# GpSimd's early work given to ScalarE and VectorE, with the maxima of the next head in three attention groups

## The reference, cut to what matters

```
x = x + gnn(layernorm(x))            # (x - mean) / sqrt(var + 1e-5)
x = x + ffn(layernorm(x))
def gat(x, W, a_src, a_dst, bias):   # per head
    h    = x @ W
    al_s = sum(h * a_src);  al_d = sum(h * a_dst)
    e    = leaky_relu(al_s[src] + al_d[dst], 0.2)
    ex   = exp(e - segment_max(e, dst)[dst])
    out  = segment_sum(h[src] * ex / segment_sum(ex, dst)[dst], dst)
# gnn: layer 1 has 4 heads of 512 and an elu, layer 2 one head of 768
# ffn: router, top 2 of 8 experts of capacity, experts and a shared expert
```

## Time and profile before

| what | value |
|---|---|
| median of 3 executions | 1455.62 us (1454.12 to 1456.59) |
| profiled execution | 1458.8 us, its span 1457.0 us |
| granted TensorE clock, mean | 0.932 |
| busy: PE, PEld | 1255.7 us (86%), 817.3 us (56%) |
| busy: DVE, ACT, POOL | 919.4 us (63%), 583.2 us (40%), 293.8 us (20%) |
| chain that ended last | PE 54%, DVE 23%, DMA 7%, ACT 6%, POOL 5%, issue 5% |

### The profile page before, as it was taken

The page is one execution under the profiler, slowest core; times in us unless marked ns, Lnnn a source line. Parts: engine busy times, 40 slices in busy tenths (PEclk is TensorE's granted clock), DMA queues, the critical chain, the costliest instruction groups (busy, mean ns, idle before and its releaser), DMA issues.

```text
span 1457.0 us, 18197 instructions
## 1 busy us (share of the span) xinstructions
PE 1255.7 (86%) x7084; PEld 817.3 (56%) x7084; DVE 919.4 (63%) x1694; ACT 583.2 (40%) x1015; POOL 293.8 (20%) x198
## 2 busy tenths in 40 slices
...
GB/s 168 53 171 167 16 56 138 112 18 102 133 109 29 110 151 96 35 64 90 41 124 188 160 86 58 42 172 43 97 66 1 63 204 183 174 193 189 174 59 29
DMA packets 71009, 151.55 MB, mean 104 GB/s; under 512 B 10789, under 2 KB 34853, under 8 KB 70298
## 3 DMA queue, kind: packets, MB, share of 16 engines
...
...
HBM read 117.78 MB, written 34.59 MB: 105 GB/s over the span
## 4 chain that ended last, share of the span: by engine, by line
PE 54%; DVE 23%; DMA 7%; ACT 6%; POOL 5%; issue 5%; SPq 1%; POOLq 0%; DVEq 0%; ACTq 0%
PE PS L1684 41%; PE PS L1812 7%; DVE sb L1327 3%; DVE sb L1254 3%; POOL sb L780 3%; DVE sb L1348 2%; DMA sb<-in_L_gnn_W_dram 2%; DVE sb L1363 2%; DVE sb L1356 2%; DMA sb<-aa_d 2%; DVE sb L1210 2%; PE PS L1714 1%; PE PS L1807 1%; DVE sb L1399 1%; DVE sb L1388 1%
## 5 line engine op out<-in xcount | busy, mean ns | idle before, releaser
L1684 PE MATMUL PS<-sb,sb 128*125 128x384 f16 (+8 forms) x4404 | 789.2, 340 | 55.9 <-DVE sb L1231 24.5
L1684 PEld LDWEIGHTS PS<-sb,sb 128*125 128x125 f16 (+3 forms) x4404 | 545.2, 129 | 286.8 <-issue 70.6
L1812 PE MATMUL PS<-sb,sb 125*128 125x375 f16 (+1 forms) x1440 | 261.0, 342 | 0.0
L1812 PEld LDWEIGHTS PS<-sb,sb 125*128 125x128 f16 x1440 | 140.0, 98 | 118.9 <-issue 8.2
L797 POOL TENSOR_TENSOR sb<-sb,sb 125x768 f32<-125x768 f32 x10 | 18.0, 1841 | 672.2 <-DMA sb<-in_x_dram 672.2
L949 ACT ACTIVATE sb<-sb 125x375 f32<-125x375 f32 (+1 forms) x150 | 81.6, 544 | 116.4 <-DVE sb L1348 116.1
L1528 DVE SCALAR_TENSOR_TENSOR sb<-sb,sb 128x2304 f16<-128x2304 f32 x27 | 68.8, 2557 | 84.3 <-ACT sb L1085 84.3
L1348 DVE SCALAR_TENSOR_TENSOR sb<-sb,sb,sb 125x375 f32<-125x375 f32 (+1 forms) x150 | 95.7, 639 | 30.6 <-ACT sb L943 30.5
L1714 PE MATMUL PS<-sb,sb 125*125 125x500 f16 x286 | 75.0, 422 | 36.1 <-ACT sb L928 23.4
L780 POOL TENSOR_TENSOR sb<-sb,sb 128x768 f32<-128x768 f32 x32 | 79.1, 2494 | 122.0 <-ACT sb L903 75.2
L943 ACT ACTIVATE sb<-sb,sb 125x375 f32<-125x375 f32 (+1 forms) x150 | 93.7, 628 | 24.2 <-DMA sb<-aa_d 24.2
...
## 6 DMA issues: line engine op xcount, KB each, us to landing
...
```

The lines of the kernel that those rows point to most:

```text
L1684: ins = M(out_, lhs(a), rhs(b), start=first and a + b == 0, stop=last and a == 1)
L1812: ins = M(PS[:, t, 0:n], hb[:, i, pa, 128 * c:128 * c + 128], P[:, i, pb, lo:lo + n], start=i == 0 and pa + pb == 0, stop=i == NT - 1 and ...
```

## The change

- GpSimd does no early work but constants: the source differences go to ScalarE, one ACTIVATE of 125x125 for each of the 171 edge columns (`differences`), the sums of W2 rows to VectorE as one multiply-and-sum of 128x768 each (`v2_sums`, 32), the lo weights of head 1 to VectorE (6).
- ScalarE normalises x, with scale and bias from VectorE (MS1 is minus mean times scale).
- Six slots for rows of W2 instead of three; the loads of head 1's weights stand ahead of `chain_row(0)` in SP's order.
- In the heads: maxima in g2, g3 and g4 (3, 3, 4) instead of two in each of g2 to g6; the shift at group 7 instead of 10; the next head's P from g9 instead of g11; W1_AT from g5 on; other counts of P calls. Masks are loaded one after the other, and the last two weight rows after the shifts.

```diff
@@ tables
-        CUR_STEPS = [[3, 3, 2, 2, 2, 2, 2, 2, 2, 0, 0, 0, 0, 0, 0],
-                     [2, 2, 2, 2, 2, 2, 2, 0, 0, 0, 0, 0, 0, 0, 0],
...
+        CUR_STEPS = [[2, 2, 2, 2, 2, 2, 2, 2, 2, 2, 0, 0, 0, 0, 0],
+                     [1, 1, 0, 0, 0, 2, 2, 2, 2, 1, 0, 0, 0, 0, 0],
+                     [1, 1, 0, 0, 0, 2, 2, 2, 2, 1, 0, 0, 0, 0, 0],
+                     [1, 1, 1, 1, 1, 2, 2, 2, 2, 0, 0, 0, 0, 0, 0]]
-        MAX_STEPS = [0, 0, 2, 2, 2, 2, 2, 0, 0, 0, 0, 0, 0, 0, 0]
+        MAX_STEPS = [0, 0, 3, 3, 4, 0, 0, 0, 0, 0, 0, 0, 0, 0, 0]
-        NEXT_STEPS = [[0, 0, 0, 0, 0, 0, 0, 0, 0, 0, 0, 2, 2, 2, 2],
...
+        NEXT_STEPS = [[0, 0, 0, 0, 0, 0, 0, 0, 0, 1, 2, 2, 2, 2, 2],
+                      [0, 0, 0, 0, 0, 0, 0, 0, 0, 1, 2, 2, 2, 2, 2],
+                      [0, 0, 0, 0, 0, 0, 0, 0, 0, 2, 3, 3, 3, 3, 3]]
+        V2_H = [0, 1, 1, 2, 1, 2, 1, 2, 2, 2]
+        V2_H1 = [0, 0, 0, 3, 1, 1, 1, 1, 1, 1]
-        W1_AT = {3: 0, 4: 1, 5: 2, 6: 3, 7: 4, 8: 5}
-        ROW_AT, SHIFT_AT = 1, 10
+        W1_AT = {5: 0, 6: 1, 7: 2, 8: 3, 9: 4, 10: 5}
+        ROW_AT, SHIFT_AT = 1, 7
@@ gpsimd: differences, products and lo weights of head 1 taken out
-            pool.wait_ge(s_slo, 1)
-            for i in range(NT):
-                a, b = OLP * i, min(OLP * (i + 1), KA)
-                nc.gpsimd.tensor_tensor(OL[:, a:b, :], iot[:, :].unsqueeze(1).to_broadcast([T, b - a, T]),
...
@@ scalar
+            def differences(q):
+                if q == 0:
+                    act.wait_ge(s_keys, 2)
+                a, b = OLP * q, min(OLP * (q + 1), KA)
+                for t in range(a, b):
+                    ins = A(OL[:, t, :], iot[:, :], ACT.Identity, bias=SLO[:, t:t + 1], scale=-1.0)
+                ins.then_inc(s_od, 1)
+
+            def normalise(n):
+                act.wait_ge(s_ms1, n + 1)
+                for i in range(*PIECES[n]):
+                    A(XA[:, i, :], XA[:, i, :], ACT.Identity, bias=MS1[:, i:i + 1], scale=SD[:, i:i + 1]
+                      ).then_inc(s_xn, 1)
+
             deviation(0)
+            normalise(0)
             deviation(1)
+            normalise(1)
+            differences(0)
...
             for i in range(NT):
+                if i == 2:
+                    differences(1)
                 if i == XF:
                     deviation(2)
+                    normalise(2)
...
             for i in range(NT):
                 h_hi(0, i)
-                if i >= 4:
-                    v2_sum(summed)
-                    summed += 1
+                if 1 <= i <= 5:
+                    differences(i + 1)
             w1_hi(1, range(KD))
 
+            for q in range(7, 9):
+                differences(q)
             for c in range(NC):
+                if c == 3:
+                    differences(9)
@@ vector
-                for i in range(a, b):
-                    V.tensor_scalar(XA[:, i, :], XA[:, i, :], MV1[:, i, 0:1], SD[:, i:i + 1], ALU.subtract,
-                                    ALU.mult).then_inc(s_xn, 1)
+                V.scalar_tensor_tensor(MS1[:, a:b], MV1[:, a:b, 0], -1.0, SD[:, a:b], ALU.mult, ALU.mult
+                                       ).then_inc(s_ms1, 1)
...
+            def v2_sums(n):
+                for k in range(summed[0], min(summed[0] + n, 2 * NCH)):
...
+                    V.tensor_tensor_reduce(VJ[:, :], WV[ch % 6][:, :], A2R[:, a, :], SW, 0.0, ALU.mult, ALU.add,
+                                           V2F[:, ch, a:a + 1]).then_inc(s_va, 1)
...
             for q in range(NT):
                 h_lo(0, q)
-                if q >= 2:
+                if 2 <= q <= 6:
                     source_onehots(q)
+                v2_sums(V2_H[q])
+            w1_lo(1, range(KD))
...
             chain_row(0)
-            pair_onehots(range(T0, ET))
+            for a in range(T0, ET, OLP):
+                for q in range(7, NT):
+                    if a <= OLP * q < a + OLP:
+                        source_onehots(q)
+                pair_onehots(range(a, min(a + OLP, ET)))
+                v2_sums(1 if a + OLP < ET else 0)
...
@@ sync
-                    load_masks(h + 1, 2)
+                    for t in range(2, 5):
+                        load_masks(h + 1, t)
                     if h + 2 < H:
                         load_al(h + 2)
                         load_w1_rows(h + 2, range(2))
-                    load_masks(h + 1, 3)
-                    load_masks(h + 1, 4)
+                    store_h1(NB * h)
                     if h + 2 < H:
-                        load_w1_rows(h + 2, range(2, KD))
-                    store_h1(NB * h)
+                        load_w1_rows(h + 2, range(2, 4))
                     chain_shift(h + 1)
+                    if h + 2 < H:
+                        load_w1_rows(h + 2, range(4, KD))
```

More of the change, by code:

```diff
@@ L133, in build @@
     MV1 = at(o_ct + 12800, [T, NT, 2], F32)
-    WV = [at(o_y + 3072 * b, [128, D], F32) for b in range(3)]
-    A2R = at(o_y + 9216, [128, 2, D], F32)
-    VP = [at(o_y + 15360 + 3072 * b, [128, D], F32) for b in range(4)]
-    assert o_y + 15360 + 4 * 3072 <= o
+    MS1 = at(o_ct + 12928, [T, NT], F32)
+    WV = [at(o_y + 3072 * b, [128, D], F32) for b in range(6)]
+    A2R = at(o_y + 18432, [128, 2, D], F32)
+    VJ = at(o_y + 24576, [128, D], F32)
+    assert o_y + 27648 <= o
     W2S = [at(o_w2s + 3072 * i, [128, 2, D], F16) for i in range(9)]
@@ L317, in build @@
         s_ml = [sem(f"masks_loaded{b}") for b in range(2)]
-        s_vp = sem("v2_product_made")
+        s_wv = [sem(f"w2_rows_in_slot{b}") for b in range(3, 6)]
         s_va = sem("v2_sum_made")
@@ L531, in _ @@
                 load_v2(ch)
-            for q in range(3, NT):
+            for q in range(3, 6):
+                load_xt(0, q)
+                load_v2(q)
+            for q in range(6, NT):
                 load_xt(0, q)
             load_w1_rows(1, range(2))
-            for ch in range(3, 8):
+            for ch in range(6, 10):
                 load_v2(ch)
@@ L582, in store_h1 @@
                                  ).then_inc(s_h1s[k % 2], 16)
+            load_w1_rows(1, range(2, KD))
             chain_row(0)
-            load_w1_rows(1, range(2, KD))
             for i in range(3):
                 load_xt(1, i)
-            for ch in range(8, NCH):
+            for ch in range(10, NCH):
                 load_v2(ch)
@@ L929, in _ @@
                   accum_out=CS[:, c:c + 1]).then_inc(s_ce, 1)
-                if c >= 4 and c % 4 < 3:
-                    v2_sum(summed)
-                    summed += 1
             def p_branch(h, b, i):
@@ L985, in y_step @@
                     act.wait_ge(s_bias, 16)
-                A(RB[:, 0:n], YB[:, y % 3, 0:n], ACT.Relu, bias=b1c[:, g:g + 1], scale=1.0 / SX
-                  ).then_inc(s_yr, 1)
+                A(RB[:, 0:n], YB[:, y % 3, 0:n], ACT.Relu, bias=b1c[:, g:g + 1], scale=1.0 / SX)
                 A(YB[:, y % 3, 0:n], YB[:, y % 3, 0:n], ACT.Exp, bias=b1c[:, g:g + 1], scale=1.0 / SX
```

68 lines of the change are left out of this document (27 added, 41 removed), and 2 rows, old and new, of the table CUR_STEPS.

## The result

The changed kernel took 1420.41 us (median of 4 executions, 1418.27 to 1423.88), the kernel before 1456.11 (4 executions, 1454.12 to 1462.13). The ratio is 0.975, 95% interval 0.9716 to 0.9785. The forecast was 1418, range 1398 to 1436. The execution that was profiled took 1423.88 us with a span of 1422.1; it is the slowest of the four, 3.5 us above their median, so a comparison of its trace with another run's can be off by as much.

What follows compares the result with a forecast made beforehand. VectorE, slowed beside GpSimd, bounds the prologue; in the heads neither TensorE nor VectorE is full. Front -23 and heads -14.3 give -37.3 on 1458.8, so 1421.5; the median lies 3.2 lower: 1418 us, range 1398 to 1436.

Steps and rivals of the forecast that it cites:

- front: Everything before the heads, from prologue to the rest of the second projection: 23 us less in sum.
- third piece; start of the projection: Prologue: VectorE's third piece of x starts at 43.0 instead of 61.89, the projection at 62.4 instead of 79.59.
- stretch of the projection: Projection of head 0: ScalarE's differences in five tiles make the last `h_lo` come 9.8 us later against the start.
- counts, to their sum: Counts stage: without GpSimd VectorE bounds it, at 64 us instead of 77.4, minus 13.
- head 0, head 1, head 2 and the rest: Heads: +0.7, -5.6 and -9.4 us, -14.3 in sum; layer 2 and the FFN 0.
- ScalarE's prices: ScalarE instructions: 0.29 us a difference, between 0.17 and 0.39; 0.92 us a normalisation, between 0.83 and 1.1.
- rival A: Front: ScalarE too slow, 0.39 us a difference, 9 us more in the projection; 1434 us in all; chance 16%.
- VectorE's account of heads 0 and 1: Heads 0 and 1: VectorE's work summed by groups; it ends at 100.2 (before 99.5) and 95.9 (before 101.5).
- The stand in g5: Head 0, group 5: TensorE stalls 13 us for P call 21 and has it back before the next projection.
- Rival C: Heads 0 to 2: the stall from bunched maxima isn't made up, +45 us less 23; 1477 us; chance 4%.
- Rival B: Heads become TensorE's as VectorE's small waits vanish: 1404 us, or 1393 with differences of 0.2 us; chance 19%.
- Rival D: Front gives nothing, weight waits and differences eat it, and heads lose their gain in g9: 1453 to 1458; chance 3%.

Runs made afterwards that it cites:

- the front alone: The changed kernel with its heads' tables, shift group and load order taken back from the kernel before: 1432.46 us, ratio 0.9839.

## Why the prediction was right, and where it was not

The forecast, 37.3 us less, met 35.7. It was right as a sum and by its mechanism; the front and the heads were off by some 4 and 6 us in opposite directions, so that the sum came within 2 us is in part luck.

| Step | Forecast | Measured |
|---|---|---|
| third piece; start of the projection | 43.0; 62.4 | 44.24; 64.44 |
| stretch of the projection | +9.8 | +9.9 (last `h_lo` 52.5 after the start, before 42.65) |
| last `h_lo` to the first chunk | +1.3 | +0.5 |
| counts, to their sum | 64, or -13 | 61.1 (140.49 to 201.56), or -16.1 |
| masks and rest of the second projection | -4 | -5.9 (sum at 222.49 before) |
| front | -23 | -26.8 |
| head 0, head 1, head 2 and the rest | +0.7, -5.6, -9.4 | +3.3, -1.8, -8.0; the two projections between, -1.7 |

*Prologue.* The third piece came 1.2 us late, since VectorE waited 1.29 us for the second piece of x at 14.29: it now came there 12 us earlier than before, and I hadn't asked whether the input was there. The 8.82 us behind it are near the 8.0 that I had for ScalarE (2.8 and 5.2). The other 0.8 us lie behind the third piece: VectorE's first split of it comes 11.7 us after the piece's start instead of 9.2, because ScalarE splits only when it has normalised all five tiles.

*ScalarE's prices* were right to 0.02 us (0.29, 0.94), so rival A falls. That the differences cost 9.8 us in the projection and stood before the first chunk was right too, and the experiment that spreads them shows that 8 us of the first and all of the second were not needed.

*Counts.* The term was too small by 3 us. I took the one-hots at the 0.41 us of the earlier trace rows; in the changed kernel, as in the last row of the run with occupied GpSimd, 18 take 6.45 us, 0.36 each. With that the sum is 57.5, and 3.7 us of waits, for TensorE at the start and for ScalarE's last chunk, make up the rest.

The means of the earlier trace rows misled me. The 4.0 us a product is the mean of one that stood for 21.10 us, while one-hots ran back to back, and eight of 1.9. Beside these the one-hots took 1.9 each too. From the timeline of the kernel before, in narrower windows:

```profile
167.72 21.10 POOL L780 TENSOR_TENSOR sb<-sb,sb 128x768 f32<-128x768 f32 x1 [6.03 <-ACT sb L903]
188.78 15.02 POOL L780 TENSOR_TENSOR sb<-sb,sb 128x768 f32<-128x768 f32 x8
192.56 11.52 DVE L1254 TENSOR_SCALAR sb<-sb,sb 125x1000 f16<-125x1000 f16 x6
```

In the whole stage 12 of 138 one-hots took 1.4 to 2.1 us beside a product, some 18 us more than their own work; in the changed kernel none did. So most of the term is the neighbour. The run with occupied GpSimd agrees: it has 13 such one-hots, and loses 20 us between first chunk and count sum (156.16 to 237.21).

*Heads.* The step that failed is VectorE's account of heads 0 and 1. VectorE's waits in head 1, from its start to tile 2 of the next projection, before and after:

```profile
DVE sb L1348 <- ACT sb L943: 11.3, 1, 11.3
DVE sb L1406 <- ACT sb L988: 3.8, 4, 1.2
DVE sb L1414 <- ACT sb L999: 1.7, 3, 0.6
DVE sb L1216 <- ACT sb L892: 0.6, 1, 0.6
```
```profile
DVE sb L1421 <- ACT sb L983: 6.5, 5, 1.4
DVE sb L1207 <- ACT sb L891: 4.2, 6, 1.0
DVE sb L1361 <- ACT sb L939: 2.4, 1, 2.4
DVE sb L1414 <- PE PS L1829: 1.5, 1, 1.5
```

The wait for the broadcast (the row with one long wait) fell by 8.9 us, as worked out. Against it stand hi weights of ScalarE 3.6 us more, since W1_AT puts them into groups where VectorE has done all else; the exponential 2.7 more, since maxima took the place of the P calls that had hidden it; TensorE's groups 1.5 more (2.3, 0.8 of it put down to issue, instead of 0.8); busy time 1.1 more; and 1.7 less for the hi part of the output. That leaves 1.7 of the 1.8 us that head 1 gave. Of these my account had the broadcast, and 1.2 us for each elu without a P call before it; it had nothing for the weights and for TensorE's groups. In head 0 the wait for weights is 4.5 us instead of 1.2, and that for TensorE's groups 4.2 instead of 1.1. Making the lo weights later took these waits away and shortened both periods.

The start of the last head, where I put most of the 25.3 us of the earlier trace rows, had 12.9 of them.

*The stand in g5* was 12.7 us (forecast 13), in g10 of head 1 3.5 and two smaller ones, 4.8 in all (5), of head 2 6.4 (no figure forecast). Rival C, that it is not given back, falls with the 0.32 us that VectorE waited behind it and the 6.95 us that TensorE stood at tile 2. Rival B falls: VectorE's waits didn't vanish, they changed their names. (Its 1404 is 1406 by its own terms, 12 off 1418.) Rival D falls with the front alone.

*Which part did it.* For the front, that GpSimd idle is the cause, and not where the instructions went, is shown: with GpSimd busy the third piece starts at 60.83 (61.89 before), and the counts are slow again. The heads give their 6 to 13 us by the tables; which of the tables does it no run separates. The half of the change that gives x to ScalarE is against it: on its own it costs some 4 us (0.975 against 0.972, intervals that overlap).
